# Turning the new unit's probabilities ahead of the fourth chunk of values, at the change of pass of a two-layer attention and aggregation kernel

## Chip, cores and metric

One core of a Trainium2 chip runs one launch of one program. The metric is the device time of that launch in microseconds (us), from the median of several runs. One further execution was recorded by the hardware profiler; its rows are what this document reads.

## What is computed

```python
q = x @ Wq.T + bq;  k = key @ Wk.T + bk;  v = value @ Wv.T + bv      # all 4096 x 512
scores = (q @ k.T) / 64 * adj                                        # 4096 x 4096
scores = where(abs(scores) < 1e-5, -1e9, scores)
x = layernorm(x + (softmax(scores) @ v) @ Wm.T + bm)
x = layernorm(x + relu((adj @ x) @ W1.T + b1))                       # returned
```

## The kernel before

Weights are merged first, so that a row block's scores come from `t = x @ Aq` and the raw keys, and the output from raw values and one product of `Wv` and `Wm`. Numbers are kept as a high and a low fp16 part, and each product is three passes of matmuls over these parts.

The attention runs in two passes over the 4096 keys and values, 2048 at a time, since only one half of the values (`V`) fits in the on-chip memory. Each pass has 32 units; a unit is 128 rows of queries (`NT` is 32, so units 0 to 31 are the first pass and 32 to 63 the second, `g` in the code). For each unit TensorE makes the scores (`scores`, L690: four chunks of 12 matmuls), VectorE and ScalarE mask them, take the maximum and the exponentials and split the probabilities in a high part (ScalarE, L937) and a low part (VectorE, L1276) in `Phl`. SyncE turns each part with one DMA transpose into `PT` (`turn_prob`, L313 for the high part and L316 for the low part; 128 x 2048 fp16, 512 KB each). Then TensorE multiplies `PT` with `V` (`weigh`, L710: 16 tiles of 3 matmuls). TensorE runs the scores of unit g+1 ahead of the weighing of unit g.

At the change of pass TensorE's order is: scores of 32, weighing of 31, scores of 33, weighing of 32, scores of 34, weighing of 33, project 32 (L731), scores of 35. The weighing of unit 31 is the last to use the first half of `V`. The second half lies in DRAM (`vp_dram`) and is loaded over it in four chunks of 1 MB (`load_second_values`, L388): chunks 0 to 2 each wait for a quarter of that weighing (`p_use`), chunk 3 for its end (`o_mm`, L387). The weighing of unit 32 waits for both turned parts (L697, L698) and, at every fourth tile, for the next chunk of `V` (L708).

SyncE's instructions run in the order written, and one that waits holds all behind it. Behind the chunks stand: the store of unit 31's output to `o_dram` (`store_first`, L320, after ScalarE's copy L942), a wait until all outputs of the first pass are stored (L432), the load of unit 32's first-pass output (`load_o`, L394), the turning of unit 32 (`turn_prob(NT, 0)`), and then `second_step` for unit 33: load `t` of unit 34 (L293), store and load some tiles, turn unit 33. ScalarE reads `t` of unit 34 at L914 ahead of the exponentials of unit 33 (L929), both in its own written order; VectorE finishes `thl` at L1220, and the scores of unit 34 wait for it (L681).

All of SyncE's transfers go through one hardware DMA queue; GpSimd issues the loads of the adjacency (`adjh`, L554) on another.

Of the kernel before, what the change touches and what calls it, by code (L numbers as in the profile page):

```python
# [30 lines left out]
def attention_then_aggregation(nc, x, adj, key, value, wq, bq, wk, bk, wv, bv, wm, bm, w1, b1, out):  # L31
# [3 lines left out]
    NT = N // P  # L35
# [3 lines left out]
    MC = HALF // C  # L39
# [21 lines left out]
    with ctx:  # L61
# [204 lines left out]
        with nc.Block() as block:  # L266

            @block.sync
            def _(sp):
# [35 lines left out]
                def scales_made():  # L305

                    sp.wait_ge(s_sig, 5)

                def turn_prob(g, b):

                    scales_made()
                    sp.wait_ge(p_hi, g + 1)
                    sp.dma_start_transpose(PT[:, b, HI, :, :], Phl[:, b, HI, :]).then_inc(ph_in[b], 16)  # L313
                    scales_made()
                    sp.wait_ge(p_lo, g + 1)
                    sp.dma_start_transpose(PT[:, b, LO, :, :], Phl[:, b, LO, :]).then_inc(pl_in[b], 16)  # L316

                def store_first(g, n, b):
                    sp.wait_ge(u_ev, g + 1)
                    sp.dma_start(o_dram[bass.ds(n * P, P), :], z_out[:, b, :]).then_inc(o_st[b], 16)  # L320
# [62 lines left out]
                def load_second_values(c):  # L383
                    if c < MC - 1:
                        sp.wait_ge(p_use, (MC - 1) * (NT - 1) + c + 1)
                    else:
                        sp.wait_ge(o_mm, NT)  # L387
                    sp.dma_start(V[:, :, c * TC:(c + 1) * TC, :], vp_dram[:, :, c * TC:(c + 1) * TC, :])\  # L388
                      .then_inc(vp_in[c], 16)

                def load_o(g, n, b):

                    wait(sp, u_lo, g - NT - 1)
                    sp.dma_start(o_in[:, b, :], o_dram[bass.ds(n * P, P), :]).then_inc(o_ld[b], 16)  # L394
# [14 lines left out]
                def second_step(n, b, j, merged, stored):  # L409

                    g = NT + n
                    if not isinstance(n, int) or n < NT - 1:
                        load_t(g + 1, n + 1)
                    store_adj(g, n, b, j, 1)
                    if stored:
                        store_z(g - 3, n - 3, 1 - b)
                    load_o(g, n, b)
                    if merged:
                        load_x(n - 1, 1 - b)
                    turn_prob(g, b)  # L420
                    if merged:
                        turn_merged(g - 1, 1 - b)
# [2 lines left out]
                load_t(NT + 1, 1)  # L425
                store_adj(NT, 0, 0, NT // 2, 1)
                sp.wait_ge(v1_st, 16 * MT)
                for c in range(MC):
                    load_second_values(c)
                store_first(NT - 1, NT - 1, 1)  # L430
                for b in range(2):
                    sp.wait_ge(o_st[b], 16 * (NT // 2))  # L432
                load_o(NT, 0, 0)
                turn_prob(NT, 0)
                second_step(1, 1, NT // 2, True, False)
                second_step(2, 0, NT // 2 + 1, True, False)
                second_step(3, 1, NT // 2 + 1, True, True)
# [1118 lines left out]
```

## Time and profile before

| | us |
|---|---|
| median of 3 runs | 2171.53 |
| lowest and highest | 2170.22, 2173.21 |
| the profiled execution | 2173.73 |
| its span, first to last instruction | 2172.1 |
| TensorE busy in it | 2108.8 (97%) |
| VectorE, ScalarE, GpSimd busy | 1211.0, 649.2, 89.7 |
| mean granted TensorE clock | 0.987 of full speed |

Times in rows are us from the start of the span. The second pass begins on TensorE at 846.27 us, with the scores of unit 32. A share of busy time says little about a stretch of 30 us, so the change is read from that stretch. The 2173.73 us is the time by which a sum made from the trace is measured; the median of the runs is 2.20 us lower.

### The profile page before, as it was taken

Reading aid. Unit: us, or ns where it says so; the run is one execution under the profiler, and the core shown is the slowest. Engines: PE = TensorE matmul, PEld = TensorE weight load, DVE = VectorE, ACT = ScalarE, POOL = GpSimd, SP = SyncE. Lnnn points to the kernel's source line nnn. Section 1 sums busy time; section 2 is a strip of 40 time slices with the busy share of each in tenths; the row PEclk is TensorE's granted clock in tenths of the full one; section 3 lists DMA queues with packets and bytes.
Section 4 is the critical chain, followed back from the end, with each engine's and each line's share of the span. In section 5 each row is a group of like instructions: output and inputs, shape, how many; then the busy total and the mean of one; then the engine's idle time right before and its main releaser. Section 6 shows DMA issues by size and latency. Waiting matters only on the chain.

```text
span 2172.1 us, 28525 instructions
## 1 busy us (share of the span) xinstructions
PE 2108.8 (97%) x9710; PEld 1035.4 (48%) x9710; DVE 1211.0 (56%) x2597; ACT 649.2 (30%) x865; POOL 89.7 (4%) x159
## 2 busy tenths in 40 slices
PE   7997999999999999999999999999979999999998
PEld 5773444444444444344444444444434554445554
DVE  3876565665656655566766767767755232122323
ACT  3343443434434434333333333333323000000000
POOL 1110000000000000000000000000000000000000
PEclk9998999999999999999999999999999999999999
DMA  6675666666666666755655655655578433344321
GB/s 237 226 264 159 170 160 168 158 172 159 159 179 159 164 179 165 180 156 135 150 155 135 150 155 135 150 155 135 140 185 221 97 95 90 87 105 102 94 66 39
DMA packets 537768, 325.12 MB, mean 150 GB/s; under 512 B 460929, under 2 KB 465025, under 8 KB 537729
## 3 DMA queue, kind: packets, MB, share of 16 engines
q1 hardware_dynamic: 516096, 245.96, 41.9%
q0 software_dynamic: 21632, 78.65, 15.6%
q8 instruction: 23, 0.38, 0.1%
q14 instruction: 17, 0.13, 0.0%
HBM read 173.55 MB, written 71.30 MB: 113 GB/s over the span
## 4 chain that ended last, share of the span: by engine, by line
PE 91%; DVE 3%; DMA 3%; ACT 1%; SPq 1%; issue 1%; DVEq 0%; ACTq 0%
PE ps L690 30%; PE ps L710 30%; PE ps L787 20%; PE ps L800 4%; PE ps L731 4%; PE ps L651 2%; DMA stg<-in_L_gnn_value 1%; DMA wc<-in_L_gnn_Wv 1%; PE ps L635 1%; DVE mcol L1115 0%; PE ps L598 0%; DMA o_dram<-z_out 0%; DMA z_in<-z_dram 0%; PE ps L664 0%; DVE agg L1524 0%
## 5 line engine op out<-in xcount | busy, mean ns | idle before, releaser
L690 PE MATMUL ps<-KT,thl 128*128 128x512 f16 x3072 | 677.8, 381 | 9.6 <-DVE thl L1220 9.6
L710 PE MATMUL ps<-V,PT 128*128 128x512 f16 x3072 | 678.1, 381 | 7.0 <-issue 7.0
L690 PEld LDWEIGHTS ps<-KT,thl 128*128 128x128 f16 x3072 | 301.5, 98 | 375.6 <-DVE thl L1220 10.4
L710 PEld LDWEIGHTS ps<-V,PT 128*128 128x128 f16 x3072 | 301.6, 98 | 373.4 <-issue 14.0
L787 PE MATMUL ps<-adjT,X 128*128 128x512 bf16 x2048 | 452.0, 379 | 2.1 <-DMA adjT<-adj_bf 1.1
L1247 DVE SCALAR_TENSOR_TENSOR prob<-ps,c_now,adjh 128x512 f32<-128x512 f32 x256 | 192.2, 751 | 306.4 <-PE ps L690 304.3
L924 ACT ACTIVATE small<-prob 128x512 f32<-128x512 f32 x256 | 161.4, 630 | 620.1 <-DVE prob L1247 331.4
L787 PEld LDWEIGHTS ps<-adjT,X 128*128 128x128 f16 x2048 | 195.8, 98 | 251.3 <-DVE agg L1524 13.8
L1276 DVE SCALAR_TENSOR_TENSOR Phl<-prob,Phl 128x2048 f16<-128x2048 f32 x64 | 146.7, 2292 | 105.9 <-ACT Phl L937 105.9
L1260 DVE CUSTOM_DVE_ANT_0 prob<-prob,small 128x512 f32<-128x512 f32 x256 | 174.0, 682 | 0.0
L929 ACT ACTIVATE prob<-prob,nbias,inv 128x2048 f32<-128x2048 f32 x64 | 134.1, 2095 | 98.9 <-DVE nbias L1269 98.9
L1253 DVE TENSOR_SCALAR small<-small,eps_s,neg_s 128x512 f32<-128x512 f32 x256 | 139.0, 543 | 23.9 <-ACT small L924 23.9
L1524 DVE TENSOR_TENSOR agg<-ps,agg 128x512 fp32r<-128x512 f32 x32 | 19.9, 683 | 219.4 <-ACT agg L1042 219.4
L937 ACT ACTIVATE Phl<-prob 128x2048 f16<-128x2048 f32 x64 | 122.3, 1910 | 7.1
L651 PE MATMUL ps<-xT,Aq 128*128 128x512 f32 x384 | 96.6, 402 | 1.8 <-DVE xT L1055 1.8
L731 PE MATMUL ps<-Wvm,UT 128*128 128x512 f16 x384 | 90.1, 385 | 8.2 <-DMA UT<-Uhl 8.2
L800 PE MATMUL ps<-WT,agg 128*128 128x512 f32 x384 | 97.8, 405 | 0.2 <-DVE agg L1524 0.2
L1485 DVE TENSOR_TENSOR y<-ps,b_rep 128x512 f32<-128x512 f32 x32 | 22.1, 691 | 135.6 <-PE ps L800 135.6
L554 POOL DMA_DIRECT2D adjh<-in_adj x64 | 34.2, 534 | 1332.0 <-DVE prob L1247 959.5
L1033 ACT ACTIVATE std<-vare 128x1 f32<-128x1 f32 x32 | 6.5, 203 | 255.8 <-DVE vare L1498 255.8
L1042 ACT ACTIVATE agg<-ps 128x512 fp32r<-128x512 f32 x32 | 16.5, 603 | 221.0 <-PE ps L787 221.0
L800 PEld LDWEIGHTS ps<-WT,agg 128*128 128x128 f32 x384 | 72.1, 188 | 18.2 <-issue 0.7
(137 smaller groups left out, 1147.2 us busy)
## 6 DMA issues: line engine op xcount, KB each, us to landing
adjh<-in_adj POOLq DMA_DIRECT2D x64, 512.0 KB, 5.3
adj_bf<-adjh SPq DMA_DIRECT2D x64, 512.0 KB, 3.9
t_in<-t_dram SPq DMA_DIRECT2D x64, 256.0 KB, 2.8
x_in<-in_x SPq DMA_DIRECT2D x64, 256.0 KB, 3.8
stg<-in_L_gnn_value POOLq DMA_DIRECT2D x12, 1024.0 KB, 8.2
rows<-in_x SPq DMA_DIRECT2D x32, 256.0 KB, 3.6
t_dram<-tq POOLq DMA_DIRECT2D x8, 1024.0 KB, 9.6
o_dram<-z_out SPq DMA_DIRECT2D x32, 256.0 KB, 2.6
```

The source lines that it names most:

```text
L651: last = nc.tensor.matmul(ps[:, BT + e, :], Aq[:, m, k, e * P:(e + 1) * P], xT[:, b, s, k, :], start=(n == 0), stop=(n == 3 * KD - 1))
L690: last = nc.tensor.matmul(ps[:, BS + c, :], thl[:, b, s, k * P:(k + 1) * P], KT[:, m, k, c * C:(c + 1) * C], start=(n == 0), stop=(n == 3 ...
L710: last = nc.tensor.matmul(ps[:, BU + b, :], PT[:, b, s, m, :], V[:, v, m, :], start=(m == 0 and q == 0), stop=(m == MT - 1 and q == 2))
L731: last = nc.tensor.matmul(ps[:, BZ + b, :], UT[:, b, s, k, :], Wvm[:, m, k, :], start=(n == 0), stop=(n == 3 * KD - 1))
L787: last = nc.tensor.matmul(ps[:, BG + d, :], X1[:, s, m, d * P:(d + 1) * P], adjT[q][:, m % QT, :], start=(m == 0 and s == HI), stop=(m == ...
L800: last = nc.tensor.matmul(ps[:, BF + k % 2, :], agg[:, u, d, k * P:(k + 1) * P], WT[:, w, d, :], start=(d == 0 and q == 0), stop=(d == KD ...
L924: nc.scalar.activation(small[:, c % 2, :], prob[:, b, c * C:(c + 1) * C], ACT.Abs).then_inc(s_abs, 1)
L929: nc.scalar.activation(prob[:, b, :], prob[:, b, :], ACT.Exp, bias=nbias[:, b:b + 1], scale=inv[:, 0:1], accum_out=rsum[:, b:b + 1]).then_ ...
L1247: nc.vector.scalar_tensor_tensor(out=prob[:, b, c * C:(c + 1) * C], in0=ps[:, BS + c, :], scalar=c_now[:, b:b + 1], in1=adjh[:, b, c * C:( ...
L1253: nc.vector.tensor_scalar(small[:, c % 2, :], small[:, c % 2, :], eps_s[:, 0:1], neg_s[:, 0:1], ALU.is_lt, ALU.mult).then_inc(s_neg, 1)
L1260: nc.vector.tensor_tensor_reduce(out=prob[:, b, c * C:(c + 1) * C], in0=prob[:, b, c * C:(c + 1) * C], in1=small[:, c % 2, :], scale=1.0, ...
L1276: nc.vector.scalar_tensor_tensor(out=Phl[:, b, LO, :], in0=prob[:, b, :], scalar=P_SCALE, in1=Phl[:, b, HI, :], op0=ALU.mult, op1=ALU.subt ...
```

## The change

One call of `turn_prob` moves up by three places in SyncE's written order. Ahead of it now stand chunks 0 to 2 of the second values only; chunk 3, the store of the first pass' last output, the wait for all those stores and the load of unit 32's first-pass output stand behind it. No instruction is added or removed, and no semaphore or count changes.

```diff
                 sp.wait_ge(v1_st, 16 * MT)
-                for c in range(MC):
+                for c in range(MC - 1):
                     load_second_values(c)
+                turn_prob(NT, 0)
+                load_second_values(MC - 1)
                 store_first(NT - 1, NT - 1, 1)
                 for b in range(2):
                     sp.wait_ge(o_st[b], 16 * (NT // 2))
                 load_o(NT, 0, 0)
-                turn_prob(NT, 0)
                 second_step(1, 1, NT // 2, True, False)
```

## Rows read from the trace of the kernel before

**Rows 1.** The page: each engine's busy share, and the ending chain by engine

```profile
PE 2108.8 (97%) x9710; PEld 1035.4 (48%) x9710; DVE 1211.0 (56%) x2597; ACT 649.2 (30%) x865; POOL 89.7 (4%) x159
...
PE 91%; DVE 3%; DMA 3%; ACT 1%; SPq 1%; issue 1%; DVEq 0%; ACTq 0%
```

**Rows 2.** The chain of waits, 830 to 940 us: start, length, what

```profile
867.65 7.12 DMA o_dram<-z_out
...
875.24 0.02 SPq L312
...
875.29 4.44 DMA PT<-Phl
879.73 2.63 issue
882.36 13.44 PE ps L710 x48
895.80 10.36 PE ps L690 x48
```

**Rows 3.** The timeline of TensorE: start, length, work, idle time before it

```profile
866.83 10.52 PE L690 MATMUL ps<-KT,thl 128*128 128x512 f16 x48
...
882.36 13.44 PE L710 MATMUL ps<-V,PT 128*128 128x512 f16 x48 [5.01 <-issue]
```

**Rows 4.** Windows: length, busy PE, PEld, DVE, ACT, POOL; clock, DMA share, GB/s

```profile
868.00:869.00 1.00, 1.00 (x7) 0.41 (x6) 0.26 (x3) 0.00 (x0) 0.00 (x0) 1.00 1.05 422
...
878.00:879.00 1.00, 0.00 (x0) 0.00 (x0) 1.00 (x4) 0.00 (x0) 0.00 (x0) 1.00 1.27 286
...
883.00:884.00 1.00, 1.00 (x3) 0.30 (x2) 0.48 (x1) 1.00 (x2) 0.00 (x0) 0.50 1.08 385
```

**Rows 5.** The timeline of SyncE's queue, 859 to 880 us: start and length of issuing

```profile
859.30 8.26 SPq L388 DMA_DIRECT2D V<-vp_dram  x4
...
875.29 2.26 SPq L313 DMA_TRANSPOSE PT<-Phl  x1
877.64 1.66 SPq L316 DMA_TRANSPOSE PT<-Phl  x1
879.35 0.57 SPq L293 DMA_DIRECT2D t_in<-t_dram  x1
```

**Rows 6.** The timeline: ScalarE and VectorE make unit 32's high and low parts

```profile
863.53 1.91 ACT L937 ACTIVATE Phl<-prob 128x2048 f16<-128x2048 f32 x1
865.48 2.29 DVE L1276 SCALAR_TENSOR_TENSOR Phl<-prob,Phl 128x2048 f16<-128x2048 f32 x1 [3.43 <-ACT Phl L937]
```

**Rows 7.** DMA issues, 855 to 885 us: count, size, median us to landing

```profile
V<-vp_dram SPq DMA_DIRECT2D x4, 1024.0 KB, 7.1
```

**Rows 8.** DMA issues near 1599.7 us, behind one another: us to landing

```profile
z_in<-z_dram SPq DMA_DIRECT2D x1, 1024.0 KB, 8.4
adjT<-adj_bf SPq DMA_TRANSPOSE x1, 13.2
```

**Rows 9.** Line L313 in the first pass, 31 transposes: to landing

```profile
DMA to landing us min/median/max: 3.7/3.7/4.2
```

**Rows 10.** The timeline behind the gap: what units 33 and 34 need

```profile
882.76 0.72 ACT L914 ACTIVATE thl<-t_in,up 128x512 f16<-128x512 f32 x1 [2.94 <-DMA t_in<-t_dram]
...
884.89 0.53 POOL L554 DMA_DIRECT2D adjh<-in_adj  x1 [26.12 <-DMA adj_bf<-adjh]
...
890.30 3.08 SPq L316 DMA_TRANSPOSE PT<-Phl  x1
```

**Rows 11.** DMA issues, 890.2 to 890.5 us: unit 33's low part, to landing

```profile
PT<-Phl SPq DMA_TRANSPOSE x1, 5.3
```

**Rows 12.** The timeline of TensorE at the end of attention: two short idles

```profile
1597.14 12.21 PE L710 MATMUL ps<-V,PT 128*128 128x512 f16 x48 [2.04 <-issue]
...
1613.06 7.07 PE L787 MATMUL ps<-adjT,X 128*128 128x512 bf16 x32 [1.12 <-DMA adjT<-adj_bf]
```

**Rows 13.** A window behind the shorter idle, columns as in rows 4

```profile
1614.00:1616.00 2.00, 2.00 (x11) 0.90 (x10) 1.90 (x5) 1.26 (x2) 0.00 (x0) 1.00 1.25 283
```

## Prediction

> **What bounds the kernel now.** I read the page first. TensorE is busy 97% of the span and carries 91% of the chain that ended last [rows 1], so only a place where TensorE stands idle, or runs at the lower clock, can give time back. Next comes the chain of waits around the change of pass. For hundreds of us it is TensorE alone, in blocks of 10.36 us, but here it leaves TensorE: the store of unit 31's output takes from 867.65 us until it has landed 7.12 us later, SyncE comes to the waits of `turn_prob` at 875.24 us, the high part is transposed from 875.29 us and lands 4.44 us later, 2.63 us more pass, and only at 882.36 us does the weighing of unit 32 begin [rows 2]. The 2.63 us called "issue" has no releaser in the profile; the low part, issued at 877.64 us [rows 5], is what the kernel waits for there, and it must have landed just before 882.36. The timeline of TensorE gives the size: the scores of unit 33 end at 877.35 us by their start and length [rows 3], and TensorE idles 5.01 us [rows 3].
>
> The gap has a second price. The weighing behind it lasts 13.44 us where a block of as many matmuls takes 10.36 us [rows 2], 3.08 us more. A window of that stretch shows the granted clock at 0.50, which is the lower level of 1.2 GHz, and counts 3 matmuls in its us where the one at full clock, 2.4 GHz, counts 7 [rows 4]; ahead of the fall the engine had been idle for 5 us. So the place costs 5.01 + 3.08 = 8.09 us against a TensorE that never waits. The transposes' data was ready long before: the high part is made at 863.53 + 1.91 = 865.44 us and the low part at 865.48 + 2.29 = 867.77 us [rows 6]. The transposes stood behind other work in SyncE's written order and for no other reason.
>
> **The change, part by part.**
>
> *The high part.* SyncE has issued chunk 2 of the values at about 864.4 us: three quarters of the weighing of unit 31, whose 10.36 us begin 10.36 us before the scores of unit 33, near 856.6 us. It now goes to the transpose and finds the data at 865.44 us, so it issues about 865.5 instead of 875.29. Its landing is another question, since the DMA engines are full: 422 GB/s, share 1.05, with the chunks [rows 4]. Each chunk lands 7.1 us after its issue [rows 7], so chunk 2 lands near 871.6. All of this goes through one queue, and I take it that the transposes move when chunk 2 has been moved.
>
> *What one transpose takes behind a full queue.* No row shows a `PT` transpose behind 1 MB copies. The nearest are at the end of attention: a 1 MB copy issued at about 1599.2 us landed 8.4 us later, at 1607.6, and a 1 MB transpose issued behind it at 1599.8 landed 13.2 us later, at 1613.0 [rows 8], so 5.3 us later than the copy, or 2.65 us for the 512 KB of one part. A second estimate: while unit 32's two transposes are the main traffic, the engines move 286 GB/s [rows 4], and 0.52 MB at that rate is 1.85 us. A third: the low part landed about 882.3 - 879.7 = 2.6 us behind the high one [rows 2]. The longest case is that each takes its full latency alone, 3.7 us [rows 9], with no overlap. I take 2.65 us, the row in which the queue was full, and keep 1.85 and 3.7 for the range.
>
> *The sum for unit 32.* High part at 871.6 + 2.65 = 874.2, low part at 876.9 us (875.3 with the low price, 879.0 with the high one). The low part can't be issued before 867.77 and so would not land before 871.5 in any case, which doesn't bind. TensorE wants it at 877.35 us. The margin is 0.5 us: thin, but on the right side. The idle time of 5.01 us goes, and with no idle time the clock has no cause to fall, so the 3.08 us go too. The two issues themselves cost nothing: SyncE does no work that TensorE waits for between 865 and 870 us.
>
> The Trainium skill says otherwise of the price: in "Advanced Engine Details and Errata", section "X-Bar Transpose (TRN2)", transposes are as fast as regular DMAs, at 350 to 400 GB/s. By that each part would take about 1.4 us as an estimate from the page and the low part would land near 874.4, with 3 us of margin instead of 0.5. This trace doesn't agree: it moves 286 GB/s with transposes where copies get 422 [rows 4]. The sum above does not use the page.
>
> *Chunk 3.* It now waits for `p_lo` at 867.77 us instead of `o_mm` at 867.01, and for two issues of about 2 us each (2.26 and 1.66 us in rows 5). In the queue it stands behind both transposes. Four chunks were issued in 8.26 us [rows 5] with equal landing times [rows 7], so a chunk is moved in about 2.6 us, and chunk 3 lands at 876.9 + 2.6 = 879.5 instead of 874.1 us. Its first user is tile 12 of 16 of the weighing, 7.8 us into it, at 885.1 us. The cover is 5.6 us: free. With the high price the chunk lands at 881.6, but the weighing then also starts later (at 879.0), and the cover is 5.2 us.
>
> *The last store, the wait for it and the load behind it.* The store landed 0.7 us behind chunk 3 before (874.77 against 874.1), so now at 880.2 us instead of 874.8. The load of unit 32's first half goes out at 880.3; VectorE uses it only after unit 33's maximum, and the merge of unit 32 can't come before its weighing ends at 887.7. What matters is what SyncE does next.
>
> *What is late next: `t` of unit 34.* Its load was issued at 879.35 us [rows 5], behind the two transposes. Those are out of the way now, but SyncE stands at the wait for the store until 880.2 and issues near 880.7, 1.35 us later than before. ScalarE began on `t` at 882.76 us [rows 10]; now at 884.1, `thl` is whole about 1.5 us later (two operations of some 0.72 us [rows 10]), at 885.6. Its user, the scores of unit 34, now starts at 877.35 + 10.36 = 887.7 instead of 895.80 [rows 2]. Margin 2.1 us.
>
> *And the turning of unit 33.* ScalarE takes the exponentials of unit 33 after `t` of unit 34, so all of it moves by the same 1.35 us. The low part was issued at 890.30 us [rows 10] and landed 5.3 us later, at 895.6 [rows 11], slowed by an adjacency load issued at 884.89 [rows 10]. Now 896.95. The weighing of unit 33 wants it at 887.7 + 10.36 = 898.1. Margin 1.1 us, and 2.5 with the low price. Before the change these 8 us of cover came from the gap itself; nothing further along is as near, since from unit 34 on a step has 23.3 us of TensorE work and its chain starts as much earlier as TensorE does.
>
> *Sum.* 8.09 us less and nothing in its place: 2173.73 - 8.1 = 2165.6 us against the profiled execution. The runs' median stands 2.2 us below that execution, so 2171.53 - 8.1 = 2163.4 us. What is measured of two kernels of this length can't be told from no change below about 0.2%, 4.3 us; this is 0.37%.
>
> **The rivals.**
>
> *A. The wait is made shorter, not removed.* The high price of 3.7 us puts the low part at 879.0 us, 1.65 us after TensorE wants it. Unit 33's low part would then land at 899.05, 2.1 us more, but would be wanted at 899.7, so the two waits don't add. For A speaks that the margins of 0.5 and 1.1 us are smaller than what I don't know of the transposes' price; against it, that this price means no overlap at all, which the 2.6 us between two landings contradicts. Does the clock fall too? After 1.12 us of idle [rows 12] the window shows full clock [rows 13]; after 2.04 us the block lasted 12.21 us [rows 12], 1.85 us over 10.36. With the idle alone the gain is 8.1 - 1.65 = 6.45 us, 2165.1 us; with the lower clock it is 4.6 us, 2166.9 us. Both are still faster, the second barely.
>
> *B. The move hardly brings the landing forward.* The transposes could share the engines with chunk 3 and the store issued behind them, not go ahead of them, and land near 881 us. Then the idle is cut to some 3.6 us, the lower clock still costs up to 3.1 us, and the gain is 1.4 us: 2170.1 us. Against it: the load of `t` was issued at 879.35, before the low part had landed [rows 5], and the low part still landed 2.6 us behind the high one.
>
> *C. Slower: the wait for the last store becomes the bound.* SyncE now stands at L432 with the load of `t` for unit 34 behind it, and unit 33's whole chain behind that. It was released at 874.8 us and I count 880.2. It decides when unit 33's weighing starts later than it did, 895.80 + 10.36 = 906.2 us, which needs its low part 9.2 us later than my 896.95, so the store landing at 889.4. That takes transposes of over 7 us each in the queue. A further 5 us beyond that point, with a lower clock of 3 us behind the idle, would give 2171.5 + 8 = 2179.5 us. Nothing in the trace shows transposes so slow; the slowest in rows here took 5.3 us beside an adjacency load, and between 865 and 877 us no such load runs.
>
> **How the numbers follow.** The forecast, with the stall gone or under 1 us: 0.73. A: 0.13, of which 0.02 would end within 0.2%. B: 0.10. C: 0.04. Faster by over 0.2%: 0.73 + 0.11 = 0.84; within 0.2%: 0.02 + 0.10 = 0.12; slower: 0.04. The likeliest is the forecast, 2163.4 us. No unknown cost reaches below it, so the low end is only what executions differ by, the 2.2 us between the profiled one and the median: 2161.2. The high end takes in both cases of A and part of the runs' spread, 2168.0.
>
> **What the changed profile would show.** Both transposes issued between 865.5 and 870 us, chunk 3 behind them. The scores of unit 33 followed by the weighing of unit 32 with no idle time, in 10.36 us, clock 1.00 throughout. The scores of unit 34 at 887.7 and the weighing of unit 33 at 898.1 us. SyncE's wait at L432 ending near 880, the load of `t` at 880.7. The chain of waits should stay on TensorE through the change of pass. I am wrong if TensorE still idles ahead of either weighing (the price of a transpose), if it waits at tile 12 (chunk 3), or ahead of the scores of unit 34 (the store). If all that holds and the time is not 8 us less, the gain was given back later, and TensorE's idle times behind 900 us would show where.

## The result, and the profile after

The changed kernel takes 2164.32 us in the median (2162.12 to 2167.15, 7 runs), the kernel before beside it 2170.71 us (2170.13 to 2173.23, 7 runs). The ratio is 0.9968, with a 95% interval of 0.9957 to 0.9980: faster by 0.32%, some 7 us (the interval is 4.3 to 9.3 us). Later runs of the same kernel against the kernel before (`e5_after_again` below) gave 0.9967 (0.9955 to 0.9979). One run of one experiment's kernel (`e4_past_two_chunks`) took 4510.98 us; no trace of it was kept, and it is left out of that kernel's ratio, though not of its median. The profiled execution took 2167.15 us with a span of 2165.6, against 2173.73 and 2172.1 before.

In the changed kernel every line from 429 on has a number one or more higher, so that L690 and L710 are now L691 and L711. The timeline of TensorE at the change of pass; before, the weighing of unit 32 stood behind 5.01 us of idle time and lasted 13.44 us [rows 3]:

```profile
856.56 10.52 PE L711 MATMUL ps<-V,PT 128*128 128x512 f16 x48
866.92 10.52 PE L691 MATMUL ps<-KT,thl 128*128 128x512 f16 x48
877.28 10.52 PE L711 MATMUL ps<-V,PT 128*128 128x512 f16 x48
888.35 10.53 PE L691 MATMUL ps<-KT,thl 128*128 128x512 f16 x48 [0.55 <-DVE thl L1221]
898.72 10.52 PE L711 MATMUL ps<-V,PT 128*128 128x512 f16 x48
```

The weighing of unit 32 (877.28) follows the scores of unit 33 without a gap and at full clock. A short idle time has come ahead of the scores of unit 34: 888.35 instead of 877.28 + 10.36 = 887.64, so 0.71 us by starts. From the start of unit 31's weighing to the start of unit 33's it is 898.72 - 856.56 = 42.16 us. In the kernel before this stretch was 906.00 - 856.47 = 49.53 us, and four blocks without any gap are 4 x 10.36 = 41.44 us. This stretch is the measure of all experiments below, since what lies ahead of it differs between the profiles by up to 4.4 us and what lies behind it by up to 1.6 us. Each stretch is read from one profile, and the two profiles of the changed kernel (`after` and `e5_after_again`) differ by 0.72 us in it.

SyncE's queue in the same stretch, start and length of issuing:

```profile
859.39 5.67 SPq L388 DMA_DIRECT2D V<-vp_dram  x3
865.61 6.71 SPq L313 DMA_TRANSPOSE PT<-Phl  x1
872.42 1.76 SPq L316 DMA_TRANSPOSE PT<-Phl  x1
874.23 0.59 SPq L388 DMA_DIRECT2D V<-vp_dram  x1
874.87 0.60 SPq L320 DMA_DIRECT2D o_dram<-z_out  x1
880.81 0.35 SPq L394 DMA_DIRECT2D o_in<-o_dram  x1
881.20 0.43 SPq L293 DMA_DIRECT2D t_in<-t_dram  x1
```

The high part is issued 9.7 us earlier than before [rows 5], but its issue lasts 6.71 us instead of 2.26. Everything behind it is held for that time. The landings, from the DMA issues around 864.5, 865.6, 872.4 and 881.2 us (the last number is us from issue to landing):

```profile
V<-vp_dram SPq DMA_DIRECT2D x1, 1024.0 KB, 8.0
...
PT<-Phl SPq DMA_TRANSPOSE x1, 8.8
...
PT<-Phl SPq DMA_TRANSPOSE x1, 3.8
...
t_in<-t_dram SPq DMA_DIRECT2D x1, 256.0 KB, 5.6
```

So chunk 2 lands at 872.5, the high part at 874.4, the low part at 876.2 and `t` of unit 34 at 886.8 us. The chain of waits, where before it went through the last store, the high part and a slow weighing [rows 2], now runs on through SyncE to `t`:

```profile
865.61 6.71 SPq L313
...
872.42 1.76 SPq L316
...
874.23 0.59 SPq L388
...
874.87 5.88 DMA o_dram<-z_out
...
881.20 5.56 DMA t_in<-t_dram
...
886.79 0.73 ACT thl L915
...
887.54 0.76 DVE thl L1221
...
888.35 10.53 PE ps L691 x48
```

All of it is one chain, but it costs TensorE 0.71 us only.

### The profile page after: what moved, and what is told of

Its sections match the earlier page's. It is cut to its first block, busy times and chain, and to the rows that moved or that the text cites. A ratio compares the mean times of both kernels' runs of the same rounds, so it can differ in the third digit from the quotient of the medians.

```text
span 2165.6 us, 28477 instructions
## 1 busy us (share of the span) xinstructions
PE 2103.8 (97%) x9662; PEld 1035.4 (48%) x9710; DVE 1210.6 (56%) x2597; ACT 650.2 (30%) x865; POOL 89.7 (4%) x159
## 4 chain that ended last, share of the span: by engine, by line
PE 90%; DVE 4%; DMA 3%; SPq 1%; ACT 1%; issue 1%; DVEq 0%; ACTq 0%
PE ps L691 30%; PE ps L711 29%; PE ps L788 20%; PE ps L801 4%; PE ps L732 4%; PE ps L652 3%; DMA stg<-in_L_gnn_value 1%; DMA wc<-in_L_gnn_Wv 1%; PE ps L636 1%; PE ps L599 0%; DVE mcol L1116 0%; SPq L313 0%; DMA z_in<-z_dram 0%; DMA o_dram<-z_out 0%; PE ps L665 0%
## 5 line engine op out<-in xcount | busy, mean ns | idle before, releaser
L691 PE MATMUL ps<-KT,thl 128*128 128x512 f16 x3072 | 678.1, 381 | 10.1 <-DVE thl L1221 10.1
L711 PE MATMUL ps<-V,PT 128*128 128x512 f16 x3072 | 673.5, 379 | 2.0 <-issue 2.0
L691 PEld LDWEIGHTS ps<-KT,thl 128*128 128x128 f16 x3072 | 301.4, 98 | 376.7 <-DVE thl L1221 11.5
L711 PEld LDWEIGHTS ps<-V,PT 128*128 128x128 f16 x3072 | 300.5, 98 | 364.7 <-issue 2.5
L1254 DVE TENSOR_SCALAR small<-small,eps_s,neg_s 128x512 f32<-128x512 f32 x256 | 139.3, 544 | 24.1 <-ACT small L925 24.0
L801 PEld LDWEIGHTS ps<-WT,agg 128*128 128x128 f32 x384 | 72.1, 188 | 18.1 <-issue 0.7
```

What stands on the lines that cost most here:

```text
L691: last = nc.tensor.matmul(ps[:, BS + c, :], thl[:, b, s, k * P:(k + 1) * P], KT[:, m, k, c * C:(c + 1) * C], start=(n == 0), stop=(n == 3 ...
L711: last = nc.tensor.matmul(ps[:, BU + b, :], PT[:, b, s, m, :], V[:, v, m, :], start=(m == 0 and q == 0), stop=(m == MT - 1 and q == 2))
L801: last = nc.tensor.matmul(ps[:, BF + k % 2, :], agg[:, u, d, k * P:(k + 1) * P], WT[:, w, d, :], start=(d == 0 and q == 0), stop=(d == KD ...
L1254: nc.vector.tensor_scalar(small[:, c % 2, :], small[:, c % 2, :], eps_s[:, 0:1], neg_s[:, 0:1], ALU.is_lt, ALU.mult).then_inc(s_neg, 1)
```

## The experiments

Each edit is shown against the kernel that its text names. "Stretch" is the time from the start of unit 31's weighing to the start of unit 33's.

| kernel | turning of unit 32 stands | idle ahead of its weighing, us | its length, us | stretch, us | ratio to before (95%) |
|---|---|---|---|---|---|
| before | behind all | 5.01 | 13.44 | 49.53 | |
| `e3_gap_filled` | behind all, gap filled | 0.60 | 10.52 | 46.95 | 0.9990 (0.9981 to 0.9999) |
| `e8_wait_split` | behind all but the wait for the last store | 3.03 | 12.21 | 46.32 | 0.9983 (0.9974 to 0.9992) |
| `e6_past_the_wait_only` | ahead of the wait and the load | 2.08 | 10.52 | 43.68 | 0.9975 (0.9963 to 0.9987) |
| `e2_past_store_only` | ahead of the store too | 1.16 | 10.52 | 42.77 | 0.9967 (0.9954 to 0.9980) |
| after | ahead of chunk 3 too | 0 | 10.52 | 42.16 | 0.9968 (0.9957 to 0.9980) |
| `e5_after_again` | the same | 0 | 10.52 | 41.44 | 0.9967 (0.9955 to 0.9979) |
| `e4_past_two_chunks` | ahead of chunk 2 too | 0 | 10.52 | 41.44 | 0.9967 (0.9954 to 0.9980) |
| `e1_t_early` | as after, `t` loaded earlier | 0 | 10.52 | 41.44 | 0.9963 (0.9950 to 0.9976) |
| `e10_gpsimd_then_turn` | behind all chunks, these by GpSimd | 2.94 | 12.21 | 46.23 | 0.9986 (0.9975 to 0.9997) |
| `e9_chunk3_by_gpsimd` | as after, chunk 3 by GpSimd | 5.55 | 13.20 | 49.82 | 0.9982 (0.9969 to 0.9995) |
| `e7_values_by_gpsimd` | first, all chunks by GpSimd | 14.69 | 12.59 | 58.36 | 1.0037 (1.0024 to 1.0051) |

**The load of `t`, moved too.** Against the changed kernel:

```diff
                 turn_prob(NT, 0)
+                load_t(NT + 2, 2)
                 load_second_values(MC - 1)
```

(and `second_step` leaves that load out for unit 33).

> The changed kernel, with the load of t for unit 34 also moved: it stands right behind the turning of unit 32, ahead of chunk 3, the last store and the wait for the stores. Theory (what is left at the change of pass is that load, held by the wait for the stores and then landing 5.6 us after its issue): it is issued near 874.2 us instead of 881.2, TensorE's idle time ahead of the scores of unit 34 (0.55 us in the row, 0.71 us by starts) is gone, the exponentials of unit 33 start near 882.4 instead of 887.4, and the weighing of unit 33 begins 8.0 us earlier than in the kernel before, not 7.3. Whole time about 2163.6 us, 0.7 us under the changed kernel. Rival (the load would be late anyway, since the engines are full until 880 us): it lands near 881 or later but the idle time stays. Rival (what bounds the end of attention is another chain): the idle time goes and the whole time does not move.

The load is issued at 874.00 us and TensorE no longer idles. Two lines of TensorE's timeline:

```profile
877.11 10.52 PE L712 MATMUL ps<-V,PT 128*128 128x512 f16 x48
887.47 10.52 PE L692 MATMUL ps<-KT,thl 128*128 128x512 f16 x48
```

The stretch is 41.44 us, all of the 8.09 us that the prediction counted. The first theory holds in the trace, and the first rival does not: the load landed 3.3 us after its issue. The gain is still there at the last weighing of the attention, which starts 732.5 us behind the start of the stretch against 733.3 in `after`. In the whole time it can't be seen: 2163.45 us (2162.22 to 2166.31), within the spread of the changed kernel's runs.

**One part of the change: past the store and its wait, not past chunk 3.** Against the kernel before:

```diff
                 for c in range(MC):
                     load_second_values(c)
+                turn_prob(NT, 0)
                 store_first(NT - 1, NT - 1, 1)
...
                 load_o(NT, 0, 0)
-                turn_prob(NT, 0)
```

> One part of the change alone: the turning of unit 32 stands behind all four chunks, but ahead of the last store and of the wait for the stores. Theory (a transpose's issue lasts until what is ahead of it in the queue has landed, and each part lands some 1.9 us behind that): high part issued at 867.7 and blocked until chunk 3 has landed at 874.2, landing near 876.2, the low part near 878.1; TensorE idles about 0.8 us ahead of the weighing of unit 32, at full clock; weighing of unit 33 about 6.5 to 7.3 us earlier than before; whole time near 2164.5. So most of the gain would come from passing the wait for the stores, and little from passing chunk 3. With my recorded price of 2.65 us a part instead: low part at 879.4, idle 2.1 us and perhaps the lower clock, whole time 2165.5 to 2167.5. Rival (passing chunk 3 is what matters): low part at 881 or later, idle over 3.5 us, lower clock, whole time 2169 to 2171.

Measured 2164.28 us (2163.43 to 2165.22), as the changed kernel. SyncE's queue and TensorE's timeline:

```profile
866.04 6.81 SPq L313 DMA_TRANSPOSE PT<-Phl  x1
872.95 1.74 SPq L316 DMA_TRANSPOSE PT<-Phl  x1
...
876.89 10.52 PE L710 MATMUL ps<-V,PT 128*128 128x512 f16 x48 [1.16 <-issue]
```

The high part was issued near the end of the issue of chunk 3, its issue again lasted until that chunk had landed, and the low part was there at 876.8 us, 1.3 us after TensorE wanted it. The first theory's 0.8 us was too small by 0.5; the recorded price of a part gave 2.1 us, too large by 0.8. That passing chunk 3 matters most is refuted: it is worth 1.3 us of the 8.1.

**The gap filled with work.** Against the kernel before:

```diff
                 scores(NT + 1, 1, 1)
+                for i in range(22):
+                    nc.tensor.matmul(ps[:, BZ, :], Wvm[:, HI, 0, 0:P], Wvm[:, HI, 0, :], start=True, stop=True)
                 weigh(NT, 0, NT // 2)
```

> The kernel before, with 22 matmuls of 128x512 added between the scores of unit 33 and the weighing of unit 32, into a bank that nothing reads; they add work and leave nothing out. They take 22 x 0.216 = 4.75 us of the 5.01 us in which TensorE idled. Theory (the 3.1 us of the slow weighing come from the idle time ahead of it): the weighing of unit 32 still starts near 882.4 us, lasts 10.5 us instead of 13.4, at clock 1.00; whole time 3 us less than before, near 2168 us. Rival (the clock falls there for another reason, or the transposes slow the weighing): it lasts 13.4 us again and the whole time stays.

```profile
865.19 10.52 PE L690 MATMUL ps<-KT,thl 128*128 128x512 f16 x48
875.55 4.91 PE L754 MATMUL ps<-Wvm 128*128 128x512 f16 x22
881.06 10.52 PE L710 MATMUL ps<-V,PT 128*128 128x512 f16 x48 [0.60 <-issue]
```

Nothing on SyncE was changed, the transposes came as late as before, and still the weighing lasts 10.52 us instead of 13.44, at a granted clock of 1.00. So the 3 us of the slow weighing belong to the idle time ahead of it, and not to the transposes or to the chunks in flight. The stretch is 2.58 us shorter, and the median 2168.89 us (2166.40 to 2171.70) against 2170.77: 2 us less for a kernel that does 22 matmuls more, with an interval of 0.9981 to 0.9999 that is just clear of no change.

**The turning two chunks up.** Against the changed kernel, `load_second_values(MC - 2)` also stands behind `turn_prob(NT, 0)`.

> The changed kernel, with the turning of unit 32 one place further up: ahead of chunks 2 and 3. Theory (a transpose's issue lasts until what is ahead of it has landed): the high part is issued at 865.6 and blocked only until chunk 1 has landed near 869.5, so for about 3.8 us, not 6.7; high part landed near 871.5, low part near 873.4; chunk 2 and chunk 3 issued near 871.4 and 872.0, landed by 879.6, in time for tiles 8 and 12 (882.5 and 885.1 us); store landed near 880.3, t of unit 34 as late as in the changed kernel. TensorE does not idle ahead of the weighing; whole time as the changed kernel's, 2164.3 within 1.5 us. Rival (the long issue of 6.7 us is the transpose's own cost beside running copies): it lasts some 6.7 us again, and the chunks are issued near 874 us, chunk 2 landing near 879 and chunk 3 near 882, still in time.

```profile
858.22 3.11 SPq L388 DMA_DIRECT2D V<-vp_dram  x2
864.44 4.28 SPq L313 DMA_TRANSPOSE PT<-Phl  x1
```

With one chunk less ahead, the issue of the high part lasts 4.28 us instead of 6.71: 2.4 us less, about what one chunk takes. The theory said 3.8. Chunk 1 landed near 868.9 us and the issue ended at 868.7, so the issue lasts until what is ahead in the queue has been moved, and is no fixed cost of a transpose beside copies. The median is 2163.42 us; nothing is gained in time, since TensorE had no idle time left there.

**The changed kernel again.**

> The changed kernel once more, for a second profile. It tells whether the landing of t of unit 34, 5.6 us after its issue in the first profile (3.3 to 4.1 in two kernels close to it), comes back. If it was that one execution's: landing 3.4 to 4.2 us, no idle time ahead of the scores of unit 34, and 41.44 us from the start of unit 31's weighing to that of unit 33's (4 x 10.36) instead of 42.16. If it belongs to the order: 5.5 us and 0.5 to 0.7 us idle again. Whole time 2164.3 within 1 us either way.

```profile
872.89 10.52 PE L711 MATMUL ps<-V,PT 128*128 128x512 f16 x48
...
877.06 0.43 SPq L293 DMA_DIRECT2D t_in<-t_dram  x1
...
881.46 0.72 ACT L915 ACTIVATE thl<-t_in,up 128x512 f16<-128x512 f32 x1 [5.94 <-DMA t_in<-t_dram]
...
883.25 10.52 PE L691 MATMUL ps<-KT,thl 128*128 128x512 f16 x48
```

This time `t` landed 4.4 us after its issue and TensorE did not idle: `thl` was whole at 883.0 us, and the scores begin at 883.25. The 5.6 us were of that one execution, but the place is close to the bound: the load took 4.1 us in `e4`, 4.4 here and 5.6 in the first profile, and at 4.4 only some 0.3 us of cover are left. The median was 2163.48 us (2162.08 to 2166.81) against 2171.77 of before.

**Only the wait passed.** Against the kernel before, `turn_prob(NT, 0)` stands directly behind `store_first`.

> A smaller part of the change alone: the turning of unit 32 stands behind all four chunks and behind the last store, and ahead only of the wait for the stores and the load behind it. Theory (the 7.1 us of waiting for the store to land were the cost; what stands in the queue costs only its own transfer): the high part is issued near 868.3, its issue lasts until the store has landed near 874.8, the high part lands near 876.9 and the low part near 878.7; TensorE idles 1.4 to 1.9 us; 42.8 to 43.4 us from the start of unit 31's weighing to that of unit 33's at full clock, against 49.5 in the kernel before and 42.8 with the store passed too; up to 1.9 us more if the lower clock comes. Whole time near 2164.5 to 2166.5. Rival (the store to DRAM itself holds the transposes up): low part at 881 or later, 46 us or more.

```profile
866.58 7.04 SPq L313 DMA_TRANSPOSE PT<-Phl  x1
873.72 1.69 SPq L316 DMA_TRANSPOSE PT<-Phl  x1
...
877.70 10.52 PE L710 MATMUL ps<-V,PT 128*128 128x512 f16 x48 [2.08 <-issue]
```

The stretch is 43.68 us, 0.3 us above the range given and far from the rival's 46. The idle time is 2.24 us by starts, just above the 1.4 to 1.9 expected, and the clock stayed full. The median is 2165.67 us (2163.10 to 2168.00).

**The wait split, the turning left in its place.** Against the kernel before:

```diff
-                for b in range(2):
-                    sp.wait_ge(o_st[b], 16 * (NT // 2))
+                sp.wait_ge(o_st[0], 16 * (NT // 2))
                 load_o(NT, 0, 0)
                 turn_prob(NT, 0)
```

and the wait for `o_st[1]` stands in `second_step(1, ...)` ahead of `load_o`.

> The kernel before in its old order, with one wait moved: ahead of the load of unit 32's first-pass output it waits for the even units' stores only (unit 32 reads unit 0's row block), and the wait for the odd units', the last store among them, stands ahead of the load for unit 33. The turning is not moved at all. Theory (the cost was that wait, not the place of the turning): the high part is issued near 869 and lands near 877.5, the low part near 879.5, a little later than with the turning moved, since the store and one load stand ahead; idle 1.9 to 2.6 us with or without the lower clock; 43.4 to 46 us from the start of unit 31's weighing to that of unit 33's; whole time 2165 to 2168. Rival (what matters is what the transposes pass): 49.5 us and 2171 as before.

```profile
867.73 7.45 SPq L313 DMA_TRANSPOSE PT<-Phl  x1
875.28 1.66 SPq L316 DMA_TRANSPOSE PT<-Phl  x1
...
879.33 12.21 PE L711 MATMUL ps<-V,PT 128*128 128x512 f16 x48 [3.03 <-issue]
```

The turning is not moved and 3.21 us are gained in the stretch, so the rival is refuted; the idle time, the stretch and the median, 2168.52 us (2166.40 to 2170.62), all lie just above the ranges of the theory. The low part was ready at 879.3 us, 1.0 us later than in `e6` measured from the start of the stretch (23.9 against 22.9 us), with one load more ahead. That made 3.2 us of idle time by starts instead of 2.2, and this time the clock fell (granted 0.50 from 881 to 883 us), which cost 1.7 us more.

**The chunks on another queue.** Against the changed kernel, GpSimd issues the four chunks, each behind the same semaphore as before, between its loads of the adjacency for units 34 and 35.

> The changed kernel with the four chunks of values issued by GpSimd, each behind the same wait, so that none stands ahead of the transposes in SyncE's queue. Theory (a transpose's issue lasts as long as its own queue is full): the high part's issue at 865.5 lasts 1.6 to 3 us, not 6.7, though the same 3 MB are in flight; it lands 5 to 6.5 us after its issue, sharing the engines, and the low part near 874; chunk 3 lands by 880. Rival (the engines as such are full, whichever queue): the issue lasts 6 us or more again. Either way TensorE does not idle ahead of the weighing of unit 32; whole time within 1.5 us of 2164.

The high part's issue at 862.97 us lasts 1.49 us, as short as the theory said, and both parts land far too late, which neither theory had. The low part's issue lasts 21.50 us, with only the high part ahead of it in SyncE's queue: it too ends when what is ahead has landed (887.1 us). The timeline of SyncE's queue and TensorE:

```profile
862.97 1.49 SPq L313 DMA_TRANSPOSE PT<-Phl  x1
865.29 21.50 SPq L316 DMA_TRANSPOSE PT<-Phl  x1
...
889.49 12.59 PE L718 MATMUL ps<-V,PT 128*128 128x512 f16 x48 [14.69 <-issue]
```

The landing of the high part, from the DMA issues around 862.9 us:

```profile
PT<-Phl SPq DMA_TRANSPOSE x1, 24.1
```

And two windows, with the columns of rows 4:

```profile
867.00:869.00 2.00, 2.00 (x11) 0.88 (x9) 0.75 (x1) 0.63 (x1) 0.00 (x0) 1.00 1.04 349
...
871.00:873.00 2.00, 2.00 (x11) 0.94 (x10) 0.68 (x2) 0.26 (x2) 0.00 (x0) 1.00 1.35 89
```

The DMA engines are shown as fully busy and move 89 GB/s here, and 65 to 140 GB/s in the windows of 2 us from 869 to 885 us, where copies alone get 422 and transposes in their own queue 286 [rows 4]. The median is 2179.55 us (2177.03 to 2181.38), slower than the kernel before. The Trainium skill, in "DMA: Bandwidth & Descriptors", section "Rules for kernel authors", says of spreading transfers over the issuing engines that it brings no bandwidth and only saves issue time. The issue of the high part agrees (1.49 us against 6.71), and no bandwidth was gained. The issue of the low part does not agree (21.50 us against 1.76), and beyond that this run lost bandwidth.

**One chunk on the other queue, and the queues kept apart.** Two kernels asked what it was: chunk 3 alone issued by GpSimd, and all four by GpSimd with `sp.wait_ge(vp_in[MC - 1], 16)` ahead of `turn_prob(NT, 0)`.

> The changed kernel with chunk 3 alone issued by GpSimd, at the same wait, so near 867.2 us; chunks 0 to 2 and the transposes stay in SyncE's queue. Theory (transposes in one queue and copies in the other slow each other, as with all four chunks on GpSimd, where the engines moved near 100 GB/s for 17 us): 1 MB instead of 4 is in the other queue, so the transposes are late by a few us, not by 13: low part 21 to 27 us after the start of unit 31's weighing (19.7 in the changed kernel), and 42 to 50 us from there to the start of unit 33's. Rival (it was the amount in flight, or that all four came from GpSimd): chunk 3 is moved while SyncE's queue still works on chunk 2, the low part is on time, 41.4 us.

> All four chunks issued by GpSimd, and SyncE waits for the last of them to land before it turns unit 32, so that transposes and GpSimd's copies are never in flight together. Theory (their running together is what cost 14.7 us of idle time): chunk 3 lands some 19 us after the start of unit 31's weighing, the high part 3.7 us and the low part 6.0 us behind it, TensorE idles 4 to 5 us, the lower clock costs 1.7 to 3.1 us more: 47 to 50 us from the start of unit 31's weighing to that of unit 33's, against 58.4 with both in flight. Rival (GpSimd's copies are that slow by themselves): chunk 3 lands 33 us after that start again, and the whole is 60 us or more.

With chunk 3 alone, the high part in the DMA issues around 865.6 us:

```profile
PT<-Phl SPq DMA_TRANSPOSE x1, 15.0
```

and TensorE's timeline:

```profile
883.02 13.20 PE L716 MATMUL ps<-V,PT 128*128 128x512 f16 x48 [5.55 <-issue]
```

The high part lands 15.0 us after its issue instead of 8.8 and the low part 26.4 us behind the start of the stretch, as the theory had it. The stretch is 49.82 us, and nothing of the gain is left in this execution. It is the slowest of eight: they spread from 2163.47 to 2173.69 us, and the median, 2167.95 us, is still 3 us under the kernel before. With transposes and GpSimd's copies kept apart, the timeline shows:

```profile
871.37 1.35 SPq L313 DMA_TRANSPOSE PT<-Phl  x1
872.81 2.59 SPq L316 DMA_TRANSPOSE PT<-Phl  x1
...
877.09 12.21 PE L719 MATMUL ps<-V,PT 128*128 128x512 f16 x48 [2.94 <-issue]
```

The last chunk lands 18.1 us after the start of the stretch (871.4 - 853.3), so GpSimd's copies are fast by themselves. TensorE idles 3.1 us by starts, not 4 to 5, and the stretch is 46.23 us, just below the 47 to 50 expected and 12 us less than with both in flight. The rival is refuted: it was their being in flight together. Why they slow each other is not settled by these runs, and none issued the copies from a third engine.

## Why the prediction was right

**The price of the place** was 5.01 us of idle time and 3.08 us of slow matmuls. Both held: with no idle time the stretch is 41.44 us, 8.09 less (`e5`, `e1`, `e4`), and with the idle time filled by other matmuls the slow part goes alone (`e3`). The 3.08 us set a length of 13.44 us against a start-to-start time of 10.36; like for like, by starts, the two parts are 5.17 and 2.92 us, with the same sum. In the same way the 1.85 us of rival A is 1.69 (12.21 against 10.52).

**The transposes' landing** was put at 874.2 and 876.9 us; it came at 874.4 and 876.2. The price of a part was 1.9 us behind chunk 2 and 1.8 behind the other part, not the 2.65 I took from the transpose of rows 8. The low end, 1.85 us from the 286 GB/s of rows 4, was right. The margin at the weighing was 1.1 us and not 0.5, so rival A was further off than I had it. Rival B, the transposes sharing the engines with chunk 3 and the store, did not arise for the high part, since chunk 3 went out only at 874.23 us, and the low part landed at 876.2 with both in flight behind it.

**The step that failed, without harm,** is that of the issues. I had them cost nothing, and chunk 3 follow "two issues of about 2 us each", near 870 us. The high part's issue lasted 6.71 us, until chunk 2 had been moved, and chunk 3 was issued at 874.23. The trace of before had a sign of it, in SyncE's timeline behind the copies of rows 8, where three issues of transposes take 18.79 us and the first alone 9.58:

```profile
1599.76 18.79 SPq L450 DMA_TRANSPOSE adjT<-adj_bf  x3
```

That the error did no harm was luck, since the cheaper transposes happened to give back what the late issue took. Chunk 3 landed at 880.0 us against my 879.5 (874.23 and 5.8 us), with 5 us of cover left, and the store at 880.8 against 880.2.

**The term that was mis-sized** is the landing of `t` of unit 34. Its load went out at 881.20 us, 0.5 later than my 880.7. I gave it 3.4 us from the row of before, and it took 5.56 in one profile and 4.4 in the other. The margin of 2.1 us became an idle time of 0.71 us in the one and 0.3 us of cover in the other. So one sign of being wrong that the prediction named did come, an idle time ahead of the scores of unit 34, though not from a late store: that landed 0.6 us later than counted, the load itself took 2.2 us more. The prediction named this load as what is late next, and that is what the chain of waits now shows.

**Unit 33.** Its low part was to land at 896.95 and be wanted at 898.1 us. It landed at 898.1 (issued 894.16, 3.9 us) and was wanted at 898.7, all of it shifted by the late `t`. Margin 0.7 us against 1.1.

**The whole time.** 2163.4 us was the forecast and 2164.32 the median, inside the range of 2161.2 to 2168.0. Of the 6.5 us by which the two spans differ, 7.37 come from the stretch; 0.09 us are lost ahead of it and 0.8 us behind it. The part behind the start of unit 33's weighing lasted 1266.1 us in the profile of before and 1266.9 in that of after. It lasted 1265.4 to 1266.3 us in the eight profiles in which the last weighing, after its 2 us of idle time, ran at the lower clock (12.21 us), as in rows 12, and 1266.9 to 1267.0 in the four in which it ran at full clock. Two lines of `after`:

```profile
1589.82 10.52 PE L711 MATMUL ps<-V,PT 128*128 128x512 f16 x48 [2.00 <-issue]
...
1606.23 8.08 PE L788 MATMUL ps<-adjT,X 128*128 128x512 bf16 x31 [3.30 <-DMA adjT<-adj_bf]
```

Here the faster weighing only reaches the wait for `adjT` sooner and idles 3.30 us there instead of 1.12 [rows 12] (2.80 to 3.30 us in the four, 0.25 to 1.92 in the eight). In `after`, `e1` and `e5` the block behind is also slow (8.08 to 8.75 us instead of 7.07); in `e6` it is not (6.85). What makes the difference between the groups is not shown, and neither is that it is the change's doing: `e6` is in the group of four, `e2` and `e4` are not. Ahead of the stretch the profiles differ as well: unit 31's weighing starts between 852.2 and 856.6 us, in kernels that are the same up to there. The two pairs of medians differ by 6.4 and 8.3 us, with intervals of 4.3 to 9.3 and 4.6 to 9.8 us: both agree with the 7.4 and 8.1 us of the stretch, and they are too wide to tell these apart or to say how the two differences above enter.

**Which of the three passed things mattered.** The prediction moved the transposes past chunk 3, the store and the wait in one sum. The runs take it apart, with one profile each and passed in this order: of 8.09 us, 5.85 come from passing the wait for the last store with the load behind it (`e6`), 0.91 more from passing the store (`e2`), and 1.33 from passing chunk 3. Rival C, that this wait would hold `t` too long, was right about the place and far off in size: SyncE left it at 880.8 us, and not at 889.4. Against C the prediction said that the slowest transpose took 5.3 us; in the trace of before one took 6.4, the high part of unit 33, which changes nothing here, but `e7` and `e9` show 24.1 and 15.0 us with copies of GpSimd in flight.

## What to carry to other kernels

In a queue written out by hand, look first for a wait for a landing that stands ahead of work whose data has long been there: moving past the wait brought 5.9 us, moving past the transfers themselves 2.2 us. Price a wait of the matmul engine with its idle time and with the slow matmuls behind it, and check what the wait that was passed holds up now. Before moving copies to another issuing engine to free a queue, check whether transposes are in flight beside them: here, with all four copies moved, that turned a gain of 8 us into a loss of 8.

## What the runs showed of the hardware that I had not expected

- The issue of a DMA transpose holds its engine until what stands ahead in the same queue has been moved: 1.35 and 1.49 us with nothing ahead (`e10`, `e7`), 4.28 us behind two chunks of 1 MB, 6.52 to 6.81 us behind three or four, 7.04 us behind four and the store (`e6`), 7.45 us with a load behind these (`e8`). For unit 32's high part the issue ended 0.1 to 0.2 us ahead of the landing of the last transfer before it (`after`, `e2`, `e4`, `e6`, `e8`). The chunks and the store were issued in 0.54 to 0.65 us each behind the same queue. In the kernels with all transfers but the adjacency in SyncE's queue, the high part lands 2.1 to 2.2 us after its issue ends, and the low part 2.0 to 2.9 us.
- Transposes in SyncE's queue and copies in GpSimd's slow each other by far more than their bytes: 65 to 140 GB/s together in `e7`, against 422 and 286 [rows 4] apart, and 24.1 us to landing for 512 KB.
- The clock after an idle time of about 2 us is not fixed by its length: the block behind 1.97 to 2.08 us of idle time at the end of attention lasted 12.21 us in eight profiles, that of before among them [rows 12], and 10.52 us in four; at the change of pass 2.08 us left it full (`e6`), and 2.94 and 3.03 us did not (`e10`, `e8`). Nor does a longer idle time make the block behind it slower: it lasted 13.44 us after 5.01 us, 13.20 after 5.55 and 12.59 after 14.69.
